# Final adds shared between VectorE and GpSimd, the two partial sums loaded group by group, one place product moved

## What is computed

```python
for e in range(32):                              # a scan in the reference
    w_e = jnp.sum(jnp.where(sel == e, rw, 0), axis=-1)
    acc = acc + (silu(x @ w_gate[e]) * (x @ w_up[e])) @ w_down[e] * w_e[:, None]
return h + acc
```

## Time and profile before

| what | us |
|---|---|
| median of 3 runs | 300.29 |
| lowest and highest of them | 299.84, 306.04 |
| the profiled execution | 299.49 |
| its span, first to last instruction | 297.2 |

### The profile page before, as it was taken

One profiled execution on the slowest core, in us unless ns is written; L12 is line 12 of the kernel. 1 busy time (PEld: TensorE's weight loads), 2 busy tenths in 40 slices (PEclk: granted clock), 3 DMA queues, 4 the chain that ended last, 5 costly groups with the idle time before them and its releaser, 6 DMA issues.

```text
span 297.2 us, 3841 instructions
## 1 busy us (share of the span) xinstructions
PE 276.4 (93%) x1159; PEld 148.8 (50%) x1159; DVE 150.8 (51%) x441; ACT 124.9 (42%) x213; POOL 132.6 (45%) x134
## 2 busy tenths in 40 slices
PE   4899999879999988999999999999999999999991
PEld 1345444445547445556546555655565556554231
DVE  2658999996898705453244332432343223114345
ACT  2348999999984303223213321332133213322101
POOL 4062211976532042373465447454754463235462
PEclk9999999999999589999999999999999999999997
DMA  7999999402979464399999999999999999995763
GB/s 245 330 421 418 381 402 391 196 0 79 414 289 309 176 205 161 108 356 330 281 321 365 307 296 365 359 341 324 375 359 317 303 345 323 303 247 77 139 179 124
DMA packets 20244, 83.65 MB, mean 281 GB/s; under 512 B 3572, under 2 KB 3700, under 8 KB 14337
## 3 DMA queue, kind: packets, MB, share of 16 engines
q1 hardware_dynamic: 12592, 66.84, 60.0%
q0 software_dynamic: 7488, 16.58, 25.0%
q10 hardware_dynamic: 146, 0.02, 0.0%
HBM read 72.34 MB, written 12.92 MB: 287 GB/s over the span
## 4 chain that ended last, share of the span: by engine, by line
PE 61%; DVE 19%; ACT 3%; issue 3%; DMA 3%; POOL 1%; POOLq 1%; DVEq 0%; ACTq 0%
PE ps L1170 28%; PE ps L1198 9%; PE ps L1201 6%; PE ps L1191 5%; DMA scrap<-token_rows,idx 3%; DVE big L1458 2%; PE ps L1223 2%; DVE stats L1342 2%; PE ps L1182 2%; PE ps L1154 2%; PE ps L1057 2%; DVE raw L1464 2%; PE ps L1226 1%; DVE hit L1640 1%; DVE scrap L1423 1%
## 5 line engine op out<-in xcount | busy, mean ns | idle before, releaser
L659 POOL DMA_INDIRECT sum<-w_t,add_idx x32 | 51.2, 1599 | 25.2 <-DVE add_idx L1649 11.2
L646 POOL DMA_INDIRECT scrap<-token_rows,idx x28 | 29.5, 1053 | 58.8 <-DVE idx L1643 29.8
L879 ACT ACTIVATE w_t<-ps 128x512 f32<-128x512 f32 x36 | 21.3, 597 | 69.7 <-PE ps L1191 67.6
L1659 DVE COPY w_t<-ps 128x256 f32<-128x256 f32 x34 | 14.4, 424 | 63.0 <-PE ps L1226 61.0
L884 ACT ACTIVATE w_t<-ps 128x192 f32<-128x192 f32 x34 | 11.2, 330 | 63.0 <-PE ps L1170 57.8
L1654 DVE SCALAR_TENSOR_TENSOR w_t<-ps,scrap,w_t 128x192 f32<-128x192 f32 x32 | 13.2, 413 | 42.3 <-ACT w_t L884 36.8
L1170 PE MATMUL ps<-ring,w_t 128*128 128x384 f32 x96 | 33.0, 487 | 0.7 <-ACT w_t L879 0.7
L564 POOL TENSOR_TENSOR root_out<-root_in,minus_half 112x1 f32<-112x1 f32 x20 | 13.1, 656 | 45.2 <-DVE root_in L1359 45.1
L1170 PE MATMUL ps<-big,w_t 128*128 128x384 f32 x88 | 30.4, 488 | 0.0
L961 PE MATMUL ps<-raw,last 128*112 128x512 f32 x64 | 30.1, 623 | 0.0
L1191 PEld LDWEIGHTS ps<-ident,scrap 128*128 128x128 f32 x144 | 21.3, 206 | 7.0 <-issue 2.2
(11 more groups left out here) (215 smaller groups left out, 475.3 us busy)
## 6 DMA issues: line engine op xcount, KB each, us to landing
big<-in_ffn SPq DMA_DIRECT2D x12, 1024.0 KB, 10.1
ring<-in_ffn SPq DMA_DIRECT2D x9, 1280.0 KB, 7.9
ring<-in_ffn SPq DMA_DIRECT2D x4, 1024.0 KB, 9.9
raw<-in_ffn SPq DMA_DIRECT2D x4, 1024.0 KB, 9.6
last<-in_ffn SPq DMA_DIRECT2D x4, 1024.0 KB, 9.7
big<-in_ffn SPq DMA_DIRECT2D x3, 1280.0 KB, 7.6
big<-in_mlp_w_in SPq DMA_DIRECT2D x2, 1536.0 KB, 17.8
big<-in_mlp_w_in SPq DMA_DIRECT2D x2, 1280.0 KB, 20.3
```

The lines of the kernel that those rows point to most:

```text
L646: nc.gpsimd.indirect_dma_start(got[:, got_at(s), :], None, rows_dram[:, :], rows_, bounds_check=TOK - 1, oob_is_err=False).then_inc(ld_got ...
L659: nc.gpsimd.indirect_dma_start(acc_dram[m.two][:, :], bass.IndirectOffsetOnAxis(ap=add_idx[:, m.eight:m.eight + 1], axis=0), y[:, m.four, ...
L879: nc.scalar.activation(x_t[:, m.two, :, :], bank(2 + m.two).rearrange("p (c t) -> p c t", c=4), ACT.Copy).then_inc(xt_ready, 1)
L1659: nc.vector.tensor_copy(h_t[:, m.two, :, :], bank(6)[:, 0:2 * P].rearrange("p (c t) -> p c t", c=2)).then_inc(ht_ready, 1)
```

## The change

Four edits, all at the end of the run but for the last, which lies in the loop over passes:

1. SP loads the two sums side by side: group 0 of `sum0`, group 0 of `sum1`, group 1 of `sum0`, and so on. It waits for both sums' scatter-adds before the first.
2. GpSimd, behind its four adds of the sums, also makes the final add of groups 0 and 1 (counted by a new semaphore `fin_pool`); VectorE makes that of groups 2 and 3 alone.
3. SP stores the groups in the order 0, 2, 1, 3.
4. The place product of the next pass's second Quad stands between the two halves of Quad b's down products.

```diff
--- before.py
+++ after.py
@@ -406,6 +406,7 @@
         spread_done = sem("spread_done")
         y_last = sem("y_last")
         both_ready = sem("both_ready")
+        fin_pool = sem("fin_pool")
         h_ready = sem("h_ready")
 
         place_done = sem("place_done")
@@ -519,10 +520,11 @@
                     load_picked(bass.ds(e, 1), s)
             for n in range(2):
                 sp.wait_ge(added[n], 16 * (NE // 2))
-                for g in range(NG):
+            for g in range(NG):
+                for n in range(2):
                     sp.dma_start(part[n][:, g, :], acc_v[n][:, g, :]).then_inc(ld_part[n][g], 16)
-            for g in range(NG):
-                sp.wait_ge(fin_ready, g + 1)
+            for g, fin, count in ((0, fin_pool, 1), (2, fin_ready, 1), (1, fin_pool, 2), (3, fin_ready, 2)):
+                sp.wait_ge(fin, count)
                 sp.dma_start(out_v[:, g, :], result[:, g, :]).then_inc(out_done, 16)
             sp.wait_ge(out_done, 16 * NG)
 
@@ -680,6 +682,10 @@
                 for n in range(2):
                     pool.wait_ge(ld_part[n][g], 16)
                 nc.gpsimd.tensor_tensor(part[0][:, g, :], part[0][:, g, :], part[1][:, g, :], ALU.add).then_inc(both_ready, 1)
+            pool.wait_ge(both_ready, 2)
+            pool.wait_ge(h_ready, 4 * n_pairs + 2)
+            for g in range(2):
+                nc.gpsimd.tensor_tensor(result[:, g, :], part[0][:, g, :], h[:, g, :], ALU.add).then_inc(fin_pool, 1)
             for i in range(2):
                 pool.wait_ge(ld_got[i], 16 * n_pairs + 16 * (NE // 8 + 1))
 
@@ -1315,8 +1321,9 @@
                 transpose_h(b)
                 place_lists(Quad(k + 1, 0))
                 down_lists(a, 1, 2)
-                down_lists(b)
+                down_lists(b, 0, 1)
                 place_lists(Quad(k + 1, 1))
+                down_lists(b, 1, 2)
                 spread_lists((a, b))
                 pe.wait_ge(h_ready, 4 * k + 8)
                 for i in range(2):
@@ -1755,7 +1762,7 @@
 
                 for g in range(NG):
                     grown(g)
-            for g in range(NG):
+            for g in range(2, NG):
                 dve.wait_ge(both_ready, g + 1)
                 dve.wait_ge(h_ready, 4 * n_pairs + (g + 1))
                 nc.vector.tensor_tensor(result[:, g, :], part[0][:, g, :], h[:, g, :], ALU.add).then_inc(fin_ready, 1)
```

## The result

| | median us | runs | ratio to before, with its 95% interval |
|---|---|---|---|
| before | 301.59 | 6 | |
| changed | 304.34 | 6 | 1.0107 [1.0060, 1.0154] |
| changed, second measurement | 304.44 | 6 | 1.0109 [1.0052, 1.0166] |

The change makes the kernel slower by some 3.2 us, about 1.1% (1.8 to 4.6 us by the first interval). That is within the 2% that the forecast gave a chance of 0.97, but the forecast of 299.7 us and its range to 301.5 missed it. Of the 4.6 us between 299.7 and 304.34, some 1.3 are the base: the kernel before has a median of 301.59 over six runs, where the forecast had three runs with 300.29. Without that shift the changed kernel would stand at 303.0, still outside the range.

The account below looks back on a forecast made before the run. The end was taken as bound by GpSimd's fourth add, VectorE's blocked final adds, then stores. A 1.2 us gain given back by GpSimd's adds made span 297.1 against 297.2; 299.7 was taken between bases 299.4 and 300.2, range 298.1 to 301.5.

Parts of the forecast that it names:

- the last of the first part: End of the kernel before: GpSimd's fourth add 291.3, VectorE's adds to 293.7, last store landed 296.8, span over 297.2.
- the wrong price of the two adds: Two final adds moved to GpSimd: 1.22 us each there for 0.60 on VectorE, giving back the 1.2 us gained.
- The blocked adds: End: VectorE and GpSimd adds with SBUF operands block each other; those left from 290.1 take 3.65 us; 0.55 with loads near 0.7.
- The side-by-side rival: Final adds: VectorE and GpSimd add at once, last store landed 295.7, 1.1 us less, 298.4; chance 0.2.
- the 1.2 us that the fourth sum add was to gain: GpSimd's fourth sum add, after the reordered loads, was to end at 290.1 against 291.3 before.
- The loads: SP's eight sum loads from 281.0: first lands after 2.9 us, each further 0.70, pairs at 284.6, 286.0, 287.4, 288.8.
- The late-load rival: Sum loads, all behind the second sum's scatter-add, land slower: 0.9 us each, 3.3 the first; +1.2 us, about 300.7; chance 0.2.
- its own mark: Sign of late loads in the profile after: the eighth load lands after 289.3, with loads starting at 281.0.
- that rival's own slowest case: Loads at the slow end, 3.7 us first and 1.07 each further: fourth add ends 293.5, time given as 301.8.
- The place product: TensorE, second place product moved earlier: costs nothing, at most 0.3 us; second gather's issue moves from 284.62 to 283.6.
- The stores' landing: SP's last output store lands 2.6 to 2.8 us after issue, near the median, where stores before took 2.3 to 3.1.

Follow-up runs that it names:

- late memset: The kernel before plus a one-column GpSimd memset nobody waits for, begun when VectorE's fourth final add is counted; 1.0128 [1.0084, 1.0172].
- no adds: The kernel before with GpSimd's four sum adds moved to VectorE ahead of the final ones, no add on GpSimd; 1.0022 [0.9997, 1.0046].

## Why the prediction was wrong

**The step that failed** is the last of the first part: "four VectorE adds ... last store issued at 293.69, landed at most 3.1 later (296.8), span over at 297.2". I took the end of the span for the end of the stores, since the two agreed. There was a second end in the same place, GpSimd's drain, 5.65 us behind its last add. Its row was there to read, and the chain of waits of the kernel before even named that instruction, with the first 1.4 of its 8.2 us:

```profile
288.72 1.38 POOLq L123
```

From this follows the wrong price of the two adds: "with nothing behind them but its waits for the gathers". Behind them was the drain. Moving GpSimd's last instruction from its fourth sum add to 3.34 us later moves the end by as much, since the stores no longer matter: expected by that 3.0 to 3.7, measured alone 3.5. The step took the stores' agreement with the span for a proof; the second profile of the kernel before, where the drain is 0.9 us later than SP, shows that the agreement was in part chance.

**The blocked adds** were right. The adds took turns, and from the fourth sum add to the last final add there were 3.34 us, where the text had 3.65 "in whatever order"; an add that had waited took 0.55 and 1.12 us in place of the 0.60 and 1.22 of the text. VectorE's part of it is shown by leaving its adds out (1.26 in place of 1.72). The side-by-side rival is out.

**The two errors add up to the miss.** From the fourth sum add to the last store, 3.73 us went by in the changed kernel's profile (294.20 to 297.93) and 2.4 before; the text had 3.65 to 4.0. So the adds make the last store some 1.3 us later behind the fourth sum add, as forecast, and two things differ: the drain ends 2.2 us after SP, which the sum left out, and the 1.2 us that the fourth sum add was to gain, which was to pay for the adds, did not come. 2.2 + 1.2 = 3.4 is the miss: -0.1 us was forecast for the span, and the time rose by 3.2. That the two meet so closely is partly luck, since the interval of the 3.2 is 2.8 us wide. The parts measured one by one don't resolve it better: adds 3.5, loads 1.1 and place product 0.4 make 5.0, with intervals of 2 to 3 us each.

**The loads** were sized too well, the second step that failed. The first landed 3.0 us after issue in the second profile (taken: 2.9), but all eight took until 9.2 us after the first issue and not 7.8: a hole of 2.1 us between two landings, of 1.8 or more (1.77 to 2.67) in each of the six profiles with side-by-side loads. The fourth sum add ended 10.7 us after the first load, where the text had 9.1; before, it ended 10.3 us after the second sum's first load in one profile and 9.1 in the other. So the 1.2 us did not come. What the loads cost by themselves is +0.4%, +0.2% and +0.3% in the three kernels that have them without GpSimd's final adds, none clear of zero, and some 1 us at best guess. The late-load rival came true by its own mark: the eighth landing was to be over 8.3 us after the first issue, and it was 9.2 (the rival's own sum has 9.6). Priced at +1.2 us, it had the sign and about the size of the loads' own part; it had 0.2 of the chance, and no drain either. The range did not even hold that rival's own slowest case, given as 301.8: a fourth add at 293.5 in place of 291.9 makes 300.7 + 1.6 = 302.3.

**The place product** costs and gives nothing that can be measured (1.0012), as predicted. The two gathers' issues start 2.3 us apart in the changed kernel and 3.3 before, so the second does go out 1 us earlier, but GpSimd's adds then wait for their loads (1.53 us before the second).

**The stores' landing** is right to the tenth: at most 2.8 us after issue where 2.6 to 2.8 was taken. The order of the stores was not tested apart from the adds.

## What to carry to other kernels

Look at what each engine does after its last useful instruction, and not only at the last transfer: a kernel ends when its latest closing instruction does. In this program that of GpSimd ends 5.6 us after its last operation or wait, so its last work should be done that much ahead of the last store's landing. Whether the 5.6 us is the same in another program, no run here shows; one row of a profile tells it. When the sum of one chain gives the span exactly, look for a second chain that gives it too before pricing a move between the two engines. And two engines whose adds take turns, as VectorE's and GpSimd's do here with both operands in SBUF, gain nothing from making them at the same time; the split that paid had one engine finished before the other began.

## What was not expected of the hardware

- GpSimd's closing DRAIN takes 5.63 us when GpSimd is idle at its issue (late memset, no adds: 5626 ns in both), and ends 5.65 us after its last add otherwise, in eleven of the twelve profiles in which that was an add (5.49 in the twelfth). ScalarE's takes 0.47 us, SP's 0.01.
- Under GpSimd's adds and VectorE's adds with both operands in SBUF, the engines alternate strictly, one instruction each, with GpSimd's next add queued right behind: 1.72, 1.71 against 1.65, 1.75 us. The Trainium skill, in SBUF — State Buffer, section "Who interferes with whom", has the lock and says that issue order decides who blocks. By that the trace agrees: at 294.75 GpSimd's add, begun at 294.15, went ahead of VectorE's next, begun at 294.67, and at 295.87 that one went ahead of GpSimd's next, begun at 295.83.
- Eight loads of 224 KB issued in a row on an empty queue land with a gap of 1.8 to 2.7 us between the second and third or the third and fourth, and of 0.4 to 1.2 elsewhere (six profiles). It stays without the gathers. Its cause is open.
